# Queries moved behind the context product, w1 and w2 staged in SBUF, eight homes for x's high parts, and GpSimd's sums in another order

## The reference

```python
Q, K, V = x @ wq.T, x @ wk.T, x @ wv.T            # 64 wide each
energy  = einsum('bnd,bne->bde', K, V)            # 64 x 64, a sum over ALL tokens
context = einsum('bnd,bde->bne', Q, energy) * sqrt(3/64)
x = layernorm(x + context @ wo.T)
h = silu((x @ w1.T) * s1) * ((x @ w2.T) * s2)     # 1024 wide
h = gelu((h @ h1.T) * g1)                         # exact gelu, 1024 x 1024
h = gelu((h @ h2.T) * g2)
x = layernorm(x + (h @ w3.T) * s3)
```

## Time and profile before

| | |
|---|---|
| median of 3 runs | 647.97 us (647.49 to 648.94) |
| the profiled execution | 647.28 us, of which the span of the profile is 645.5 us |
| TensorE busy | 635.5 us, 98% |
| VectorE, ScalarE, GpSimd busy | 491.1, 411.0, 280.6 us |
| granted TensorE clock | 0.999 of full speed |
| chain that ended last | TensorE 97% |
| DMA | 103.89 MB, mean 161 GB/s; 400 GB/s and more in parts of the first 100 us |

### The profile page before, as it was taken

The page is one execution under the profiler, slowest core; times in us unless marked ns, Lnnn a source line. Parts: engine busy times, 40 slices in busy tenths (PEclk is TensorE's granted clock), DMA queues, the critical chain, the costliest instruction groups (busy, mean ns, idle before and its releaser), DMA issues.

```text
span 645.5 us, 9171 instructions
## 1 busy us (share of the span) xinstructions
PE 635.5 (98%) x3147; PEld 531.1 (82%) x3148; DVE 491.1 (76%) x722; ACT 411.0 (64%) x697; POOL 280.6 (43%) x225
## 2 busy tenths in 40 slices
PE   8989999999999999999999999999999999999996
PEld 6768887888789888888889888888889888888896
DVE  5687799989565996789665898698754899488477
ACT  6579688868672566558661757656763466666655
POOL 0376999492001762096000564078000367069025
PEclk9999999999999999999999999999999999999999
DMA  8999889953310056434330036734330015534301
GB/s 342 391 367 401 321 333 354 378 205 130 133 67 0 2 163 229 162 131 147 129 116 1 1 97 191 251 118 159 130 131 1 0 20 188 184 131 144 118 1 67
DMA packets 24370, 103.89 MB, mean 161 GB/s; under 512 B 2224, under 2 KB 3312, under 8 KB 16496
## 3 DMA queue, kind: packets, MB, share of 16 engines
q1 hardware_dynamic: 24032, 102.98, 45.1%
q10 hardware_dynamic: 288, 0.26, 0.1%
HBM read 87.51 MB, written 23.07 MB: 171 GB/s over the span
## 4 chain that ended last, share of the span: by engine, by line
PE 97%; DVE 1%; issue 0%; POOL 0%; POOLq 0%; ACT 0%; DVEq 0%
PE ps L1395 63%; PE ps L1338 18%; PE ps L1464 8%; PE ps L1487 1%; PE ps L1270 1%; PE ps L1204 1%; PE ps L1232 1%; PE ps L1258 1%; PE ps L1246 1%; PE ps L1220 1%; PE ps L1252 0%; PE ps L1239 0%; DVE st L1125 0%; DVE xr L1132 0%; POOL rstd L512 0%
## 5 line engine op out<-in xcount | busy, mean ns | idle before, releaser
L1395 PE MATMUL ps<-R,ring 128*128 128x512 f32 x1792 | 410.2, 390 | 0.2 <-issue 0.2
L1395 PEld LDWEIGHTS ps<-R,ring 128*128 128x128 f32 x1792 | 335.2, 188 | 69.9 <-issue 0.6
L984 DVE TENSOR_TENSOR R<-quarter,R 128x512 fp32r<-128x512 f32 x284 | 262.0, 946 | 58.8 <-ACT R L709 58.5
L709 ACT CAST R<-quarter 128x512 fp32r<-128x512 f32 x284 | 173.2, 616 | 30.0 <-POOL quarter L540 12.0
L1338 PE MATMUL ps<-x1T,w 128*128 128x512 f32 x512 | 119.1, 391 | 0.6 <-issue 0.5
L755 ACT ACTIVATE quarter<-U,sc 128x512 f32<-128x512 f32 x96 | 69.5, 724 | 73.7 <-DVE U L1011 28.3
L1338 PEld LDWEIGHTS ps<-x1T,w 128*128 128x128 f32 x512 | 95.4, 188 | 21.9 <-ACT quarter L755 0.9
L530 POOL TENSOR_TENSOR quarter<-quarter,quarter 128x512 f32<-128x512 f32 x32 | 50.4, 1576 | 95.0 <-ACT quarter L755 88.3
L673 ACT ACTIVATE sg<-ps,sc 128x512 f32<-128x512 f32 x64 | 44.2, 690 | 63.6 <-PE ps L1338 63.5
L481 POOL TENSOR_TENSOR ve<-mv,eps 128x4 f32<-128x4 f32 x14 | 5.6, 403 | 180.4 <-DVE mv L961 180.4
L725 ACT COPY U<-ps 128x512 f32<-128x512 f32 x96 | 56.2, 585 | 28.7 <-PE ps L1395 28.5
(11 more groups left out here) (97 smaller groups left out, 389.1 us busy)
## 6 DMA issues: line engine op xcount, KB each, us to landing
ring<-combos SPq DMA_DIRECT2D x56, 1024.0 KB, 4.9
combos<-unit SPq DMA_DIRECT2D x8, 1024.0 KB, 8.5
unit<-in_h1T SPq DMA_DIRECT2D x4, 1024.0 KB, 14.6
xr<-in_x_rows SPq DMA_DIRECT2D x8, 512.0 KB, 5.1
unit<-in_h2T SPq DMA_DIRECT2D x4, 1024.0 KB, 8.7
xT<-in_xT SPq DMA_DIRECT2D x7, 512.0 KB, 7.7
out<-xr SPq DMA_DIRECT2D x7, 512.0 KB, 3.0
w<-w_dram SPq DMA_DIRECT2D x3, 1024.0 KB, 9.3
```

Source lines behind the costliest of these rows:

```text
L709: nc.scalar.copy(R[slot_of(p, u)][:, 0, c, :], quarter[operand_home(p, u)][:, c, :]).then_inc(hi_done, 1)
L984: nc.vector.tensor_tensor(r[:, 1, c, :], quarter[operand_home(p, u)][:, c, :], r[:, 0, c, :].bitcast(f32), ALU.subtract).then_inc(lo_done, 1)
L1395: last = nc.tensor.matmul(ps[:, bank + j, :], w, view(R[slot_of(p, u)][:, part, k, :]), start=n in (0, 1, 5) and k == 0 and part == 0, sto ...
```

## The change

- **Queries.** Before the T1 product TensorE now runs only block 0's queries, block 1's, and the high half of block 2's. Block 2's low half and block 3 follow T1, blocks 4 to 7 follow block 0's attention. The banks in PSUM change to suit. Five matmuls on zeros (`WARM_MIDDLE`) are gone.
- **Homes.** `xhi` has eight homes instead of four (the new four lie in `ring`), `kv` four instead of two. ScalarE copies two blocks of `kv` (5 and 6), which VectorE did.
- **w1, w2.** They are loaded to `w12_stage` in SBUF (where U lies later) and copied from there to `w12`; the bits are summed on the stage, ahead of T1s instead of behind it. Units 3 and 4 lie on the stage, so their loads wait for the copies and the bits. Unit 0's load goes ahead of w1's.
- **Checks and GpSimd.** The bits of unit 1 move behind block 7's query copy, those of units 2 and 3 to silu 2 and 3 of block 0, the sums of unit 0 to silu 0 and 1. GpSimd does all of `combine(2)` behind `inverse_deviation(0, 1)`, without the wait for the normalisation. `flag_out(1)` stands ahead of the residual sums, not between statistics and normalisation.

```diff
-BIT_ORDER = [("wkv", 0), ("wq", 0), ("whole", 0), ("w12", 0), ("w12", 1), ("whole", 1), ("whole", 2), ("sums", 0), ("whole", 3),
-             ("sums", 1), ("whole", 4), ("sums", 2), ("sums", 3), ("whole", 5), ("sums", 4),
+BIT_ORDER = [("wkv", 0), ("wq", 0), ("whole", 0), ("w12", 0), ("w12", 1), ("whole", 1), ("sums", 0), ("whole", 2), ("whole", 3),
+             ("whole", 4), ("sums", 1), ("sums", 2), ("sums", 3), ("whole", 5), ("sums", 4),
...
-        xhi = [over(f"xhi{i}", x1T_at + 4096 * i, [P, EC, BLK], f32r) for i in range(4)]
+        xhi = [over(f"xhi{f}", x1T_at + 4096 * f if f < 4 else ring_at + 4096 * (f - 4), [P, EC, BLK], f32r) for f in range(NB)]
+
+        w12_stage = over("w12_stage", u_at, [P, 2 * EC * HID])
...
-                sp.dma_start(w12_dram[:, at:at + EC * HID], (w1_in, w2_in)[i]).then_inc(w12_relayed[i], 16)
+                sp.dma_start(w12_stage[:, at:at + EC * HID], (w1_in, w2_in)[i]).then_inc(w12_staged[i], 16)
...
-                sp.wait_ge(w12_relayed[i], 16)
-                sp.dma_start(w12[:, at:at + EC * HID].bitcast(f32), w12_dram[:, at:at + EC * HID]).then_inc(w12_in[i], 16)
+                sp.wait_ge(w12_staged[i], 16)
+                sp.dma_start(w12[:, at:at + EC * HID].bitcast(f32), w12_stage[:, at:at + EC * HID]).then_inc(w12_in[i], 16)
...
+                if 3 <= i <= 4:
+                    sp.wait_ge(w12_in[i - 3], 16)
+                    sp.wait_ge(bits_done, n_bits("w12", i - 3))
...
-            relay_w12(0)
-            relay_w12(1)
             load_unit(0)
+            stage_w12(0)
+            stage_w12(1)
             load_rows(0)
             load_w12(0)
             load_w12(1)
...
-            combine_first(2)
             inverse_deviation(0, 1)
-            pool.wait_ge(norm_done[0], 1)
-            combine_second(2)
+            combine(2)
...
-            raw_q(4)
+            copy_kvt(6)
+            copy_kv(5)
+            copy_kvt(7)
+            copy_kv(6)
+            for i in range(2):
+                bits_of_w12(i)
             act.wait_ge(t1_ready, 1)
             nc.scalar.activation(T1s[:, 0, :], ps[:, 3, 0:E], ACT.Copy, scale=CTX_SCALE).then_inc(t1_hi, 1)
-            for i in range(2):
-                bits_of_w12(i)
-            bits_of_whole(1)
+            hi_of_q(1)
+            raw_q(2)
+            raw_q(3)
+            raw_q(4)
             for q in range(ACT_TILES[0]):
                 normalise_tile(0, 0, q, q + 1, tile_norm[0])
             raw_q(5)
             raw_q(6)
+            raw_q(7)
+            bits_of_whole(1)
             hi_of_transposed(0, 6)
-            raw_q(7)
             act.wait_ge(cst_in, 16 * NCST)
             for j in range(HC):
                 silu(0, j, A)
-                if j == 0:
-                    bits_of_whole(2)
+                if j <= 1:
+                    bits_of_sums(0, range(j, j + 1))
                 if 2 <= j <= 3:
-                    bits_of_sums(0, range(j - 2, j - 1))
+                    bits_of_whole(j)
...
-            normalised_tilewise(0, 0, attention_residual, lambda: flag_out(1))
+            normalised_tilewise(0, 0, attention_residual)
+            lo_of_q(1)
             lo_of_transposed(0, 6)
...
-                q_pieces(range(20, 24), view)
+                q_pieces(range(10, 16), view)
                 pe.wait_ge(qlo_done, 1)
+                flag_sum(1)
                 for q in range(TPB):
                     attention_tile(0, q, ps[:, q, 0:E]).then_inc(op_tile, 1)
-                q_pieces(range(24, 28), view)
-                pe.wait_ge(q_raw, 2)
-                keep_clock(WARM_MIDDLE, 7)
-                pe.wait_ge(tile_sum[0], 1)
-                flag_sum(1)
-                q_pieces(range(28, 32), view)
+                q_pieces(range(16, 32), view)
```

More of the change, by code:

```diff
@@ L143, in build @@
         flag = sb("flag", [1, FLAGS], i32)
-        kv = [over(f"kv{i}", q_at + 2048 * i, [P, BLK]) for i in range(2)]
+        kv = [over(f"kv{i}", q_at + (0, 2048, 8192, 10240)[i], [P, BLK]) for i in range(4)]
         wkv = over("wkv", q_at + 4096, [P, EC, 2 * D])
@@ L149, in build @@
         ET = over("ET", q_at + 6144, [D, 2, D])
-        zeros = over("zeros", q_at + 8192, [P, BLK], mybir.dt.bfloat16)
+        kvT = [over(f"kvT{i}", q_at + 12288 + 2048 * i, [P, BLK]) for i in range(2)]
+        zeros = over("zeros", q_at + 6656, [P, BLK], mybir.dt.bfloat16)
         q_stage = [over(f"q_stage{i}", q_at + 3 * 8192 + 2048 * i, [P, BLK]) for i in range(NB - 4)]
@@ L183, in build @@
         xf_in = [sem(f"xf_in{i}") for i in range(4)]
-        w12_relayed = [sem(f"w12_relayed{i}") for i in range(2)]
+        w12_staged = [sem(f"w12_staged{i}") for i in range(2)]
         w12_in = [sem(f"w12_in{i}") for i in range(2)]
@@ L373, in _ @@
             store_unit(0)
+            relay_hidden(0, 0)
             store_q(4)
-            relay_hidden(0, 0)
-            load_unit(4)
-            store_unit(1)
             store_q(5)
@@ L380, in _ @@
             store_q(7)
-            store_unit(2)
+            load_unit(4)
+            store_unit(1)
             load_ring(0)
             relay_hidden(0, 1)
+            store_unit(2)
             store_unit(3)
@@ L393, in _ @@
             relay_hidden(1, 0)
+            load_ring(5)
             load_rows_late(3)
@@ L610, in high_x @@
                     act.wait_ge(x_first, 16)
-                if f >= 4:
-                    act.wait_ge(q_ready, f - 3)
-                nc.scalar.copy(xhi[f % 4].rearrange("p c (t n) -> p c t n", t=TPB), tiles_of(xT[f])).then_inc(xhi_done, 1)
+                nc.scalar.copy(xhi[f].rearrange("p c (t n) -> p c t n", t=TPB), tiles_of(xT[f])).then_inc(xhi_done, 1)
             def bits_of_w12(i):
-                act.wait_ge(w12_in[i], 16)
-                bits(low_halves(w12[:, i * EC * HID:(i + 1) * EC * HID]), 0, i)
+                act.wait_ge(w12_staged[i], 16)
+                bits(low_halves(w12_stage[:, i * EC * HID:(i + 1) * EC * HID]), 0, i)
             def bits_of_whole(i):
@@ L1093, in _, with copy_kv @@
             nc.vector.memset(zeros[:, :], 0.0).then_inc(zeros_made, 1)
-            for f in range(NB):
+            def copy_kv(f):
                 dve.wait_ge(kv_ready, f + 1)
-                if f >= 2:
-                    dve.wait_ge(et_ready, f - 1)
-                nc.vector.tensor_copy(kv[f % 2][:, :], ps[:, KV_BANK[f], :]).then_inc(kv_out, 1)
-                if f == 0:
-                    low_x(0)
-                    flag_out(0)
-                elif f == 1:
-                    low_x(2)
-                    low_x(1)
-                    low_x(3)
-                    low_x(4)
-                    lo_of_q(0)
-                elif f <= 4:
-                    if f == 4:
-                        lo_of_q(1)
-                    low_x(f + 3)
+                if f >= 4:
+                    dve.wait_ge(et_ready, f - 3)
+                nc.vector.tensor_copy(kv[f % 4][:, :], ps[:, KV_BANK[f], :]).then_inc(kv_out, 1)
+            copy_kv(0)
+            low_x(0)
+            flag_out(0)
+            copy_kv(1)
+            for f in range(2, 5):
+                low_x(f)
+            for f in range(5, NB):
+                low_x(f)
+                copy_kv(f - 3)
+            lo_of_q(0)
+            low_x(1)
+            copy_kv(7)
             dve.wait_ge(et_ready, NB)
@@ L1117, in _, with normalised_tilewise @@
                                            ALU.mult, ALU.subtract).then_inc(t1_lo, 1)
-            def normalised_tilewise(ln, b, add, between=None):
+            flag_out(1)
+            def normalised_tilewise(ln, b, add):
                 y = xr[:, b % 4, :].rearrange("p (t e) -> p t e", e=E)
@@ L1127, in normalised_tilewise @@
                     nc.vector.bn_aggr(mv[ln][:, ln, q, :], st[ln][:, ln, q, :]).then_inc(tile_aggr[ln], 1)
-                if between is not None:
-                    between()
                 for q in range(ACT_TILES[ln], TPB):
@@ L1222, in kv_products, with kv_copied @@
                 last.then_inc(kv_ready, 1)
+            def kv_copied(f):
+                if f in KV_ACT:
+                    return (act_kv_out, KV_ACT.index(f) + 1)
+                return (kv_out, f + 1 - sum(i < f for i in KV_ACT))
             def kv_transposed(f, view):
-                if f > 2:
-                    pe.wait_ge(kv_out, f - 2)
+                if f >= 3:
+                    pe.wait_ge(*kv_copied(f - 3))
                 for part in range(2):
```

85 lines of the change are left out of this document (40 added, 45 removed).

## The result

The changed kernel takes 649.66 us (median of 20 runs, 648.21 to 650.43), the kernel before took 647.98 beside it (20 runs, one of which took 2259 us and doesn't move the median). The ratio is 1.0023, interval [1.0017, 1.0030]: slower by 1.5 us by the ratio and by 1.7 us in the medians, where I forecast 647.2 and a range up to 649.2. The profiled execution took 649.68 us; its span is 647.9 us against 645.5.

What follows compares the result with a forecast made beforehand. TensorE bounds the kernel, busy 635.5 of 645.5 us. The front's -2.25 and a new wait's +1.45 make -0.8 us, on the median 647.97 a forecast of 647.2 us, range 645.3 to 649.2.

Steps and rivals of the forecast that it cites:

- The front: The stretch up to the start of `l1(0)`, where TensorE's waiting could be cut; forecast 2.25 us shorter.
- T1 near 26.8: Fewer query matmuls ahead of the T1 product: it starts about 2.1 us sooner than 28.91.
- The third normalisation at 0.39 us: Block 0's layer norm: the last of three normalisations takes 0.39 us instead of 1.35, as `combine(1)` starts later.
- The 2.25 us: Block 0's high part: the cast of `x1T` starts at 35.7 against 37.96, and the first silu moves with it.
- `flag_out(1)` leaves this path: nothing: Block 0's layer norm: moving `flag_out(1)` gains nothing, as the last tile waited for its deviation anyway.
- The new wait: In `l1(0)`, TensorE waits 1.45 us at block 1's transposes, since three of four normalisations each wait for a GpSimd addition.
- S: The start of the first silu, 40.52 in the kernel before; times in the following stage are counted from it.
- full collision (B): Rival: GpSimd's addition comes ahead of all four normalisations of block 1, TensorE waits 2.7 us; 648.0 to 648.5; chance 0.13.
- the middle case: The forecast itself: block 1's first normalisation runs, three wait for one addition each, TensorE waits 1.45 us; chance 0.40.
- The clock at nothing: The sum held no cost for TensorE's clock; its fall was priced only as a separate rival.
- Rival D: Without the matmuls on zeros a longer gap halves TensorE's clock; three slow tiles of `l1(0)` cost 2.8 us, 650.0; chance 0.02.
- The copies (C): Rival: copies inside SBUF take twice 3 us per MB, unit 1 lands at 39, 651.5 us; chance 0.09.

Runs made afterwards that it cites:

- run 2: The changed kernel with 13 extra matmuls, results unread, ahead of TensorE's transposes of block 1; 648.33 us, ratio 1.0015 to the kernel before.
- Experiment 8: The changed kernel with GpSimd's wait put back and six query matmuls moved back ahead of T1; 645.80 us, ratio 0.9970 to the kernel before.
- Experiment 4: The kernel before with the bits of unit 1 moved behind block 6's query copy; 647.06 us, ratio 0.9996.
- runs 7 and 3: 7: the changed kernel with the wait put between the second and third addition of `combine(2)`, ratio 0.9973; 3: the kernel before without its wait, 1.0027.
- run 1: The changed kernel with GpSimd's wait for block 1's normalisation put back ahead of `combine(2)`; 644.72 us, ratio 0.9955 to the kernel before.
- run 6: The changed kernel with the bits of units 2 and 3 behind silu 3 and 4, and no wait; 645.05 us, ratio 0.9959 to the kernel before.

## Why the prediction was wrong

**The front was right.** T1 near 26.8: 27.05, and 26.52 in run 2, which has no row of TensorE waiting for x. First residual sum 29.6: 29.99. The third normalisation at 0.39 us: 0.41, ending at 35.5 where I had 35.0. Cast at 35.7: 36.06. The 2.25 us measure 1.90 in the profile after, where x cost 0.7 in one wait; run 2, with none, had `l1(0)` 0.54 sooner still. Experiment 8 puts 0.6 to 1 us of it on the queries.

**"`flag_out(1)` leaves this path: nothing" was wrong in its reason.** Experiment 4 suggests that the flag was nearly as late as the third normalisation before, so that the two had to go together. The change did both, and the sum was not touched. I also read the earlier trace rows wrong: the 0.7 us stand there against ScalarE's normalised tile, but that tile was done at 35.68 (35.09 + 0.59) and the transposes began at 36.44, so TensorE wasn't waiting for it.

**"The new wait" is the step that failed.** GpSimd's start was right: S + 5.52 forecast, 44.15 - 38.62 = 5.53. The normalisations were not: I had S + 5.24, the trace has 44.25 - 38.62 = 5.63. Gate 2, which they follow, started at S + 4.96 instead of 4.57. I carried the distance from silu 0 to gate 2 over from the old trace. From gate 2 on the 0.67 held. Why gate 2 lies 0.39 further from silu 0 isn't settled, but it isn't TensorE, whose name its row bears: the last matmul of gate 2's tile ends at 43.05, S + 4.44, as before (44.98, S + 4.46), and silu 2 ended at 42.97. Gate 2 starts 0.53 us behind its tile with the change and 0.11 behind it before. The extra 0.4 us stand in all eleven profiles of the changed kernel and its variants and in none of the three of the old order. Two starts that I put 0.28 us apart changed places, and with GpSimd first all four normalisations waited. Within the kernel this order isn't chance: in the seven of these eleven profiles in which GpSimd isn't held ahead of its first addition, it is first by 0.10 to 0.15 us. That is the case I priced at 2.7, full collision (B), and gave 0.13; it measures 3.10. I even wrote that each piece was fixed "and they leave no slack" as a reason for the middle case, though a lead of 0.28 us in a sum of nine pieces is close to a coin's toss between 1.45 and 2.7.

**"The clock at nothing" failed with it.** Rival D looked for a gap left by the matmuls on zeros and for three slow tiles at 2.8 us. The fall came instead behind the new wait, and cost 1.1 (medians) to 1.6 us (traces). The forecast treated the wait and the clock as two independent cases; they are one. A wait of 1.05 or 1.27 us kept the clock in the profiles of runs 7 and 3, 2.07 lost it in some executions, 3.10 in all three profiles of the changed kernel. Of its 43 executions four show a mean clock of 0.999 or more, and they took 647.8 to 648.5 us.

**The sum** in the traces is -1.9 for the front, +3.2 up to the transposes and +1.6 for the clock, +2.9, and the flag's product stands 66.01 - 63.04 = 2.97 later. (The 3.2 are the wait of 3.10 and 0.13 for the first transpose, which before started while the last matmul was still running.) Behind it 0.6 comes back (spans +2.4). Before, then after, in stretches of 50 us; the second number is TensorE's busy time:

```profile
60.00:110.00 50.00, 49.78 (x221) 40.34 (x220) 45.30 (x43) 41.84 (x73) 47.26 (x30) 1.00 0.93 338
...
160.00:210.00 50.00, 49.46 (x264) 42.31 (x263) 28.99 (x51) 26.64 (x44) 2.73 (x3) 1.00 0.19 64
```

```profile
60.00:110.00 50.00, 50.00 (x223) 40.83 (x222) 47.18 (x45) 41.79 (x74) 46.44 (x30) 1.00 0.89 326
...
160.00:210.00 50.00, 49.71 (x265) 42.48 (x264) 28.56 (x52) 26.84 (x44) 1.21 (x2) 1.00 0.19 64
```

In these two stretches TensorE is idle for 0.22 + 0.54 = 0.76 us before, 0.29 after and 0.30 in run 1. That is most of why the kernel with the wait put back gains 2.6 us in span where its front gains 2.0. I had put nothing behind the collision and wasn't looking there.

**The collision's size.** Each normalisation that meets an addition ends with it: four additions from 44.15 to 49.5, four normalisations until 49.6. I had reckoned (four waits, about 10.8 behind S) the same way, and the trace has 44.25 + 5.38 - 38.62 = 11.0. GpSimd isn't slowed: its additions take 1.26 to 1.29 us and follow each other as in the kernel with the wait put back. The Trainium skill, SBUF — State Buffer (Who interferes with whom), says that VectorE's `tensor_scalar` on SBUF can run in a mode that uses a second pair of ports, which GpSimd shares, that whichever of the two issues first has the pair for its whole instruction, and that issue order decides who is blocked. The trace agrees: 0.41 us alone (35.12), 5.38 / 4 = 1.34 when GpSimd is first, and the gate at 47.14 in run 6, which reads PSUM and one tile of SBUF, keeps its 0.75 us beside an addition. No row shows the ports or the mode themselves.

**The copies (C) were not slow.** Unit 1 landed at 33.1, forecast 33, though the two copies inside SBUF took 6.6 us each from issue to landing, more than the 3 us per MB of my sum: they were under way together, with the loads queued behind them.

## What to carry to other kernels

A wait that looks like a brake may be what keeps two engines from meeting. Before taking one out, work out who arrives first, count it from the instruction that each arrival hangs on and not from a common landmark, and where the difference is smaller than what the estimate can be off, price both orders. Then ask what TensorE's clock does in the longer wait, and put the two in one case. Moving the cause of the other engine's start by one operation (run 6) was as good as the wait (run 1).

## What the hardware showed that I had not expected

- TensorE's granted clock kept its upper level behind waits of 1.05 and 1.27 us, fell behind 2.07 us in about five of eleven executions (one of them profiled), and behind 3.10 us to 0.50 for some 3 us. Thirteen matmuls whose result nobody reads, at the start of that wait, kept it at 1.00.
- Where the flag is late, TensorE goes on only 1.13 to 1.68 us behind its end (35.01 to 36.26 in run 4), shown in runs 3 and 4 only as "issue". The read of the flag and the branch stand there. With seven such reads in a kernel that is worth a look.
- One VectorE operation at one place of the program, gate 2 of block 0, starts 0.5 us behind its last operand in every profile of the changed kernel and its variants, and no row names the cause.
- Two profiles of the changed kernel differ by 1.9 us at T1 (27.05, 28.90). In the later one block 0 of x lets TensorE go on 0.7 us later (6.04 against 5.36), and the 28 products of the first two blocks that follow take 5.4 us instead of 3.7.
